# A mixture-of-experts layer's spare block: 64 rows with high and low parts side by side in place of 128 rows in three passes

## The reference

```python
xn = layernorm(x)                                   # x: (4, 1024, 512), 4096 rows
x + attention(xn) + moe(xn)

# moe: 8 experts, top 2 of softmax(xn @ Wg); capacity C = 1280 rows an expert
dispatched = xr[dispatch_mask.reshape(-1) % S].reshape(E, C, d)
h = jax.nn.relu(jnp.einsum('ecd,edf->ecf', dispatched, w1))      # d = 512, f = 2048
expert_out = jnp.einsum('ecf,efd->ecd', h, w2)
out = jnp.einsum('ks,ksm->sm', combine_weights, rerouted)
```

## Time and profile before

| | us |
|---|---|
| median of 3 runs | 2025.3 |
| lowest, highest | 2024.24, 2025.47 |
| profiled execution, its own time | 2021.71 |
| its span, first to last instruction | 2020.0 |
| TensorE busy | 2002.4 (99%) |
| VectorE busy | 906.2 (45%) |
| ScalarE busy | 553.9 (27%) |
| GpSimd busy | 722.8 (36%) |

### The profile page before, as it was taken

One profiled execution on the slowest core, in us unless ns is written; L12 is line 12 of the kernel. 1 busy time (PEld: TensorE's weight loads), 2 busy tenths in 40 slices (PEclk: granted clock), 3 DMA queues, 4 the chain that ended last, 5 costly groups with the idle time before them and its releaser, 6 DMA issues.

```text
span 2020.0 us, 29149 instructions
## 1 busy us (share of the span) xinstructions
PE 2002.4 (99%) x11768; PEld 1655.5 (82%) x11768; DVE 906.2 (45%) x1792; ACT 553.9 (27%) x986; POOL 722.8 (36%) x600
## 2 busy tenths in 40 slices
PE   9999999999999999999999999999999999999998
PEld 7888888878888888888888888888888888888887
DVE  8777677767752234224333422432352235324311
ACT  6322232223242123123212312321242124123211
POOL 4545544554442324323232431332143214333311
PEclk9999999999999999999999999999999999999999
DMA  6112121202341124215233421521152116223121
GB/s 201 68 64 86 39 69 64 86 28 80 127 151 29 44 60 143 43 58 114 66 68 70 132 44 54 125 67 35 47 146 54 28 47 160 44 63 86 56 32 21
DMA packets 85506, 151.46 MB, mean 75 GB/s; under 512 B 18304, under 2 KB 18304, under 8 KB 85360
## 3 DMA queue, kind: packets, MB, share of 16 engines
q1 hardware_dynamic: 61312, 105.64, 16.2%
q0 software_dynamic: 24048, 43.76, 12.5%
HBM read 109.82 MB, written 39.53 MB: 74 GB/s over the span
## 4 chain that ended last, share of the span: by engine, by line
PE 97%; DVE 1%; issue 0%; DMA 0%; SPq 0%; POOL 0%; ACT 0%; DVEq 0%; POOLq 0%
PE bank L1266 48%; PE bank L1570 34%; PE bank L1402 4%; PE bank L1320 2%; PE bank L1625 2%; PE bank L1391 2%; PE bank L1273 1%; PE bank L1385 1%; PE bank L1355 1%; PE bank L1294 1%; PE bank L1365 1%; DVE stats L891 0%; DMA attn_raw<-in_L_attn_Wv 0%; DMA x_in<-in_L_attn_x 0%; PE bank L1414 0%
## 5 line engine op out<-in xcount | busy, mean ns | idle before, releaser
L1213 DVE SCALAR_TENSOR_TENSOR h_lo<-bank,h_hi 128x512 fp32r<-128x512 f32 x254 | 175.3, 690 | 738.4 <-ACT h_hi L848 703.3
L637 POOL DMA_INDIRECT gathered<-xn_rows,gather_row x304 | 321.3, 1057 | 474.2 <-DVE x_blocks L1068 293.1
L1266 PE MATMUL bank<-xT_hi,w_hi 128*128 128x512 f32 x1024 | 399.1, 390 | 0.6 <-issue 0.5
L1266 PE MATMUL bank<-xT_hi,w_lo 128*128 128x512 f32 x1024 | 398.7, 389 | 0.0
L1266 PE MATMUL bank<-xT_lo,w_hi 128*128 128x512 f32 x1024 | 398.7, 389 | 0.0
L1570 PE MATMUL bank<-w_hi,h_hi 128*128 128x512 f32 x1016 | 395.6, 389 | 0.0
L1570 PE MATMUL bank<-w_hi,h_lo 128*128 128x512 f32 x1016 | 395.5, 389 | 0.0
L1570 PE MATMUL bank<-w_lo,h_hi 128*128 128x512 f32 x1016 | 395.5, 389 | 0.0
L848 ACT ACTIVATE h_hi<-bank 128x512 fp32r<-128x512 f32 x254 | 151.7, 597 | 789.5 <-PE bank L1266 744.6
L650 POOL DMA_INDIRECT out_rows<-y,add_row x80 | 128.9, 1611 | 546.7 <-ACT y L841 473.1
L1266 PEld LDWEIGHTS bank<-xT_hi,w_hi 128*128 128x128 f32 x1024 | 192.3, 188 | 41.8 <-issue 2.0
(11 more groups left out here) (217 smaller groups left out, 2324.6 us busy)
## 6 DMA issues: line engine op xcount, KB each, us to landing
raw_weights<-in_L_ffn_w SPq DMA_DIRECT2D x256, 256.0 KB
x_in<-in_L_attn_x SPq DMA_DIRECT2D x32, 256.0 KB
xn_rows<-xn SPq DMA_DIRECT2D x32, 256.0 KB, 2.8
x_res<-in_L_attn_x SPq DMA_DIRECT2D x32, 256.0 KB
out_rows<-y_attn SPq DMA_DIRECT2D x28, 256.0 KB
gathered<-xn_rows,gather_row POOLq DMA_INDIRECT x304
out_rows<-y,add_row POOLq DMA_INDIRECT x80, 5.7
attn_raw<-in_L_attn_Wq SPq DMA_DIRECT2D x4, 256.0 KB, 5.2
```

The source lines that it names most:

```text
L637: pool.indirect_dma_start(xg[:, nth % 2, q * P:(q + 1) * P], None, xn_pieces, bass.IndirectOffsetOnAxis(ap=gather_row[:, col, q:q + 1], ax ...
L1213: v_.scalar_tensor_tensor(lo[:, 0:n * P], h_bank[f % 2][:, 0:n * P], 0.0, hi[:, 0:n * P].bitcast(F32), ALU.max, ALU.subtract).then_inc(S[" ...
L1266: last = mm(dest, at(left[l], t), at_r(right[r], t), start=(i == 0), stop=(i == n - 1))
```

## The change

The first spare block now covers 64 rows. Its rows are kept as `x_halves`: for each of two halves of the tile, 64 columns of high parts and 64 columns of low parts side by side, one stationary operand of 128 columns. One pass with the high weights and one with the low weights give, in the two halves of the bank's partitions, the products of the high and of the low parts (so low by low is computed too). ScalarE copies the bank without the Relu, TensorE turns it as before, VectorE adds the two halves (a reduce over pairs, into `x_blocks`), ScalarE takes the Relu of the sum as high part, VectorE the rest as low part, both written side by side into `h_hi`, and the down product again takes two passes. Of its output bank, ScalarE scales the partitions 64 to 127 and VectorE scales the others and adds.

The second spare block is entered past 1088 rows in place of 1152. It does the other 64 rows of the first tile in the same way (`half_spare`), and then the second tile's 128 rows with three passes as before (`whole_spare`), into bank 1. It has two scatters. The gates and row numbers of the first tile are also stored with the partition halves swapped.

```diff
+HALF = P // 2
+PIECES = {1: FCHUNKS, 2: 2 * FCHUNKS}
+Y_SLOTS = [[0, 1, 2, 3], [0], [0, 1], [0, 1, 2, 3]]
...
+            if j == 1:
+                x_halves = esb("x_halves", [P, 2, DT, 2 * HALF], F32R)
...
-            return done + [(f"spare_y_by_act{k}", e + (0 < k < j)) for k in range(1, LAST)]
+            return done + [(f"spare_y_summed{k}", e + (k < j)) for k in range(1, LAST)] + [("spare_tile_out", e + (j == LAST))]
...
+            first = slot_gate[:, COLUMN[1]:COLUMN[1] + 1]
+            return (first[near, :], swapped_gate[far, :]) if j == 1 else (swapped_gate[near, :], first[far, :])
...
+        def half_cols(h, part):
+            return x_halves[:, h, :, part * HALF:(part + 1) * HALF].rearrange("p t (q c) -> p t q c", q=QUADS // 2)
+        def half_blocks(h):
+            return by_k_tile(x_blocks)[:, :, h * QUADS // 2:(h + 1) * QUADS // 2, :]
+        def by_part(ap):
+            return ap.rearrange("p (f part s) -> p f part s", f=FPC, part=2)
+        def h_sum(c):
+            return x_blocks[:, c % 2 * FPC * HALF:(c % 2 + 1) * FPC * HALF].rearrange("p (f s) -> p f s", f=FPC)
...
+                    col = COLUMN[1] if j == 1 else SLOT_TILES
+                    pool.wait_ge(S[f"spare_y_summed{j}"], e + 1)
+                    pool.indirect_dma_start(out[:, :], bass.IndirectOffsetOnAxis(ap=add_row[near, col:col + 1], axis=0),
+                                            y[near, 0, :], None, compute_op=ALU.add).then_inc(y_added[0], 16)
+                    if j == 2:
+                        col = COLUMN[2]
+                        pool.wait_ge(S["spare_tile_out"], e + 1)
+                        pool.indirect_dma_start(out[:, :], bass.IndirectOffsetOnAxis(ap=add_row[:, col:col + 1], axis=0),
+                                                y[:, 1, :], None, compute_op=ALU.add).then_inc(y_added[1], 16)
...
-                for i in range(BLOCKS[j]):
-                    uses = [sum(n > i for n in BLOCKS[:k]) for k in (j + 1, len(BLOCKS))]
+                for i in Y_SLOTS[j]:
+                    uses = [sum(i in slots for slots in Y_SLOTS[:k]) for k in (j + 1, len(BLOCKS))]
...
+                if j == 1:
+                    a.copy(half_cols(0, 0), half_blocks(0))
+                    a.copy(half_cols(1, 0), half_blocks(1)).then_inc(S["xT_hi_made"], 1)
...
-                            act.wait_ge(S[f"spare_h_done{j}"], FCHUNKS * e + c + 1)
-                            a.activation(xg[:, c % 2, :], h_bank[c % 2][:, :], ACT.Relu).then_inc(S[f"spare_h_ready{j}"], 1)
+                            act.wait_ge(S[f"spare_h_done{j}"], first + c + 1)
+                            a.copy(xg[:, c % 2, :], h_bank[c % 2][:, :]).then_inc(S[f"spare_h_ready{j}"], 1)
                         if c > 0:
-                            wait(act, (f"spare_turned{j}", FCHUNKS * e + c))
-                            a.copy(h_hi[(c - 1) % 2][:, :], xt_bank[(c - 1) % 2][:, :]).then_inc(S[f"spare_hi_made{j}"], 1)
-                    rows_out(j)
-                expert_blocks(act, e, main, spare, (("spare_h_ready", FCHUNKS), ("spare_hi_made", FCHUNKS), ("spare_y_by_act", 1)))
+                            wait(act, (f"spare_h_summed{j}", FCHUNKS * e + c))
+                            a.activation(by_part(h_hi[(c - 1) % 2][:, :])[:, :, 0, :], h_sum(c - 1), ACT.Relu
+                                         ).then_inc(S[f"spare_hi_made{j}"], 1)
+                    act.wait_ge(S["add_rows_ready"], e + 1)
+                    wait(act, (f"spare_y_done{j}", j * e + 1), ("adds_over", len(BLOCKS) * e + j))
+                    a.activation(y[near, 2, :], y_bank[0][far, :], ACT.Copy, scale=half_gates(j)[1]).then_inc(S[f"spare_far_out{j}"], 1)
...
+                if j == 1:
+                    v_.tensor_tensor(half_cols(0, 1), half_blocks(0), half_cols(0, 0).bitcast(F32), ALU.subtract)
+                    v_.tensor_tensor(half_cols(1, 1), half_blocks(1), half_cols(1, 0).bitcast(F32),
+                                     ALU.subtract).then_inc(S["xT_lo_made"], 1)
...
-                        v_.tensor_scalar(spare_used[:, 1, :], taken[0:1, :], float(MAIN + P), None, ALU.is_gt).then_inc(S["spare_known"], 1)
+                        v_.tensor_scalar(spare_used[:, 1, :], taken[0:1, :], float(MAIN + HALF), None, ALU.is_gt).then_inc(S["spare_known"], 1)
...
+                            v_.tensor_copy(swapped_gate[far, :], slot_gate[near, COLUMN[1]:COLUMN[1] + 1])
+                            v_.tensor_copy(swapped_gate[near, :], slot_gate[far, COLUMN[1]:COLUMN[1] + 1])
+                            v_.tensor_copy(add_row[near, SLOT_TILES:], slot_rec[far, COLUMN[1], 0:1])
+                            v_.tensor_copy(add_row[:, 0:SLOT_TILES], slot_rec[:, :, 0]).then_inc(S["add_rows_ready"], 1)
...
+                def half_spare(j):
+                    first = PIECES[j] * e
+                    for c in range(FCHUNKS):
+                        h_both, turned = by_part(h_hi[c % 2][:, :]), by_part(xt_bank[c % 2][:, :])
+                        dve.wait_ge(S[f"spare_turned{j}"], first + c + 1)
+                        v_.tensor_reduce(h_sum(c), turned.rearrange("p f part s -> p f s part"), AX.X, ALU.add
+                                         ).then_inc(S[f"spare_h_summed{j}"], 1)
+                        dve.wait_ge(S[f"spare_hi_made{j}"], first + c + 1)
+                        v_.scalar_tensor_tensor(h_both[:, :, 1, :], h_sum(c), 0.0, h_both[:, :, 0, :].bitcast(F32),
+                                                ALU.max, ALU.subtract).then_inc(S[f"spare_lo_made{j}"], 1)
+                    dve.wait_ge(S[f"spare_far_out{j}"], e + 1)
+                    v_.scalar_tensor_tensor(y[near, 0, :], y_bank[0][near, :], half_gates(j)[0],
+                                            y[near, 2, :], ALU.mult, ALU.add).then_inc(S[f"spare_y_summed{j}"], 1)
...
-                            product(h_bank[c % 2][:, :], (xT_hi[j], xT_lo[j]), (w1_hi[c], w1_lo[c]), DT,
-                                    slab).then_inc(S[f"spare_h_done{j}"], 1)
+                            for t in range(DT):
+                                for w in (w1_hi, w1_lo):
+                                    last = mm(h_bank[c % 2][:, :], x_halves[:, j - 1, t, :], w[c][:, t, :],
+                                              start=(t == 0 and w is w1_hi), stop=(t == DT - 1 and w is w1_lo))
+                            last.then_inc(S[f"spare_h_done{j}"], 1)
...
                             for f in range(FPC):
+                                for w in (w2_hi, w2_lo):
+                                    last = mm(y_bank[0][:, :], h_hi[d % 2][:, f * P:(f + 1) * P], w[d][:, f, :],
+                                              start=(d == f == 0 and w is w2_hi), stop=(d == FCHUNKS - 1 and f == FPC - 1 and w is w2_lo))
+                    last.then_inc(S[f"spare_y_done{j}"], 1)
```

More of the change, by code:

```diff
@@ L270, in expert_blocks @@
                 with eng.Else():
-                    for name, count in skipped:
-                        eng.sem_inc(S[f"{name}{1 + i}"], count)
+                    for name, count in skipped(1 + i):
+                        eng.sem_inc(S[name], count)
             main(LAST)
@@ L307, in evicted, with half_gates @@
             done = [("y_by_act", main_added(BY_ACT, e, j)), ("y_by_dve", main_added(BY_DVE, e, j))]
-            return done + [(f"spare_y_by_act{k}", e + (0 < k < j)) for k in range(1, LAST)]
+            return done + [(f"spare_y_summed{k}", e + (k < j)) for k in range(1, LAST)] + [("spare_tile_out", e + (j == LAST))]
+        near, far = slice(0, HALF), slice(HALF, P)
+        def half_gates(j):
+            first = slot_gate[:, COLUMN[1]:COLUMN[1] + 1]
[8 more added lines that the diff above has]
+            return x_blocks[:, c % 2 * FPC * HALF:(c % 2 + 1) * FPC * HALF].rearrange("p (f s) -> p f s", f=FPC)
         def split_units(j, f, follows):
@@ L480, in _ @@
             for i, s in enumerate(y_added):
-                sp.wait_ge(s, 16 * EXPERTS * sum(n > i for n in BLOCKS))
+                sp.wait_ge(s, 16 * EXPERTS * sum(i in slots for slots in Y_SLOTS))
         @block.gpsimd
@@ new lines, in half_spare, with whole_spare @@
+                    act.wait_ge(S["add_rows_ready"], e + 1)
+                    wait(act, (f"spare_y_done{j}", j * e + 1), ("adds_over", len(BLOCKS) * e + j))
+                    a.activation(y[near, 2, :], y_bank[0][far, :], ACT.Copy, scale=half_gates(j)[1]).then_inc(S[f"spare_far_out{j}"], 1)
+                def whole_spare():
+                    first = PIECES[2] * e + FCHUNKS
+                    for c in range(FCHUNKS + 1):
+                        if c < FCHUNKS:
+                            act.wait_ge(S["spare_h_done2"], first + c + 1)
+                            a.activation(xg[:, c % 2, :], h_bank[c % 2][:, :], ACT.Relu).then_inc(S["spare_h_ready2"], 1)
+                        if c > 0:
+                            wait(act, ("spare_turned2", first + c))
```

(35 more changed lines are left out.)

66 lines of the change are left out of this document (44 added, 22 removed).

## The result

| | before | after |
|---|---|---|
| median, us (runs) | 2025.11 (6) | 2014.47 (6) |
| lowest, highest | 2024.24, 2026.53 | 2012.0, 2016.3 |
| ratio, 95% interval | | 0.9943 [0.9932, 0.9953] |
| profiled execution, span | 2021.71, 2020.0 | 2012.0, 2010.3 |
| TensorE busy, matmuls | 2002.4, 11768 | 1982.4, 11672 |

Faster, by 10.6 us: half of the 21.4 that the prediction gave, and 6 us above the upper end of its range.

A forecast was written before the change was run, and what follows sets the result against it. TensorE's streaming of matmul columns was taken to bound the kernel. Terms of -21.8 for matmuls and +0.3 for the chain gave -21.4 us (unrounded terms), so 2000.3 profiled and 2004.0 us timed, range 2000.5 to 2008.5.

The forecast's parts named there:

- Matmuls of a used block: Two passes in place of three in both projections: 32 fewer matmuls, 7.25 us less per used block, 21.8 for three.
- The chain behind a turn: VectorE reduce, ScalarE Relu, VectorE subtract after TensorE's transposes: last chunk waits 0.1 us a block, 0.3 in all.
- rival A: The reduce is slow and TensorE waits on that chain: 2.7 us in place of 0.3, 2006.4 us; chance 0.08.
- The block's end: ScalarE copies half the output bank's partitions, VectorE adds the rest; TensorE needs the bank later: cost nothing.
- small steps: In every expert, splitting the first spare block's turned rows adds about 0.2 us each on ScalarE and VectorE: cost nothing.
- one more scatter: GpSimd issues one more scatter per expert, 1.55 us and 0.3 between two, under cover: cost nothing.
- Skipped blocks: TensorE's jumps over unused spare blocks, 80 + 192 matmuls and turns for 2 x 112: taken as 0, at most 4 us.
- Rival B: Longer jumps stall TensorE: 2008 us at 0.5 us more in eight experts, 2020 at 2 us each; chance 0.06.
- Rival D: TensorE pays for the removed pass elsewhere, something else closing the block; half the gain kept, 2014 us; chance 0.03.
- From the profile to the median: Timed median 3.6 us above the profiled execution; the same difference added to 2000.3 gives 2003.9 us.
- no new hole in experts 3, 0, 4 and 5 at the jump beyond 0.1 us: Sign of being right: TensorE shows no added idle time beyond 0.1 us at those experts' jumps over spare blocks.
- the two signs of being wrong: Blocks shrink to 16.5 us but the span falls by less than 19 us; or the reduce reads 1 us or more.

The follow-up runs named there:

- before_again: The kernel before, unchanged, profiled and timed a second time: 2025.31 us, ratio 0.9998.
- before_one: The kernel before without the second spare block's code, its semaphores counted up unconditionally: 2024.36 us, ratio 0.9991.
- before_long: The kernel before with 48 never-executed matmuls added to the second spare block, 544 instructions jumped over: 2033.39 us, ratio 1.0036.
- before_hints: The kernel before with the second block's test nested in the first's code and hints on both TensorE branches: 2004.8 us, ratio 0.9992.
- after_again: The changed kernel, unchanged, profiled and timed a second time: 2012.53 us, ratio 0.9935 to the kernel before.
- after_one: The changed kernel without the second spare block's code, its semaphores counted up unconditionally: 2001.85 us, ratio 0.9885 to the kernel before.
- after_hints: The changed kernel with the second block's test nested in the first's code and hints on both TensorE branches: 1983.88 us, ratio 0.9889.
- before_longer: The kernel before with 112 never-executed matmuls added to the second spare block, 672 instructions jumped over: ratio 1.0053.
- after_nested: The changed kernel with the second block's test inside the first block's code, so unused blocks take one jump: 2012.61 us, ratio 0.9934.
- after_hint: after_nested with TensorE's outer branch written by hand and hinted ahead of the main block's last matmuls: 2007.01 us, ratio 0.9904.

## Why the prediction was wrong

The timed span splits in three: until the first spare block starts, from there to TensorE's last matmul without the holes, and the holes.

| profile | first block at | rest without holes | holes |
|---|---|---|---|
| before | 635.43 | 1376.8 | 1.0 |
| before_again | 639.21 | 1376.7 | 1.5 |
| before_one | 639.47 | 1376.3 | 0 |
| before_long | 639.85 | 1376.9 | 7.1 |
| before_hints | 619.89 | 1376.3 | 0 |
| after | 639.49 | 1355.8 | 8.3 |
| after_again | 638.24 | 1356.0 | 10.5 |
| after_one | 637.11 | 1355.0 | 0 |
| after_hints | 619.97 | 1355.4 | 0.5 |

(After: the last matmul starts at 2003.58, and 2003.58 - 639.49 - 8.3 = 1355.8.)

- *Matmuls of a used block*: right. 96 matmuls fewer, 7.11 us a block; the middle column falls by 20.7 to 21.3 us in its four pairs (before and after, again, one, hints).
- *The chain behind a turn*: right. 0.11 us where 0.1 was given; the reduce took 0.69 us for the 0.68 of its nearest row, so rival A did not happen.
- *The block's end, small steps, one more scatter*: right at nothing. No wait of TensorE after names a scatter or the half tile's copies; VectorE's new step took 0.74 us for 0.69.
- *Skipped blocks*: this step failed. I wrote "I take 0: expert 3 shows that the jump as such can be free". Measured: 8.3 and 10.5 us of holes in place of 1.0 and 1.5, so 7 to 9 us more; my upper bound of 4 us came from one hole of 0.5 us at the old distance. What the runs show in the place of a free jump is a wait for code: TensorE goes on 1.8 to 2.3 us after a packet of 256 instructions has landed, and at the new distance a second packet can stand behind the first. A row of the old length says nothing of a longer jump when the cost comes in a step, and the step lies just there, between 496 and 544. The rule that I had put beside it and not priced in, of a stall when a branch leaves a window of two blocks of 256 instructions (the Trainium skill, "Runtime: NRT & Kernel Launch", section "Instruction fetch mechanics"), gives an estimate for the step: a jump over more than 512 instructions always leaves the window. The runs agree with it for jumps over both blocks; the larger buffer for TensorE that the same section gives does not show here. Rival B had the mechanism, at 0.06. Its near price (0.5 us each, 2008) was too low and its far one (2 us in all eight experts, 2020) too high: six places at 1.4 us each on average in the first profile. Rival D names 2014 us, almost the measured time, but that is luck: its mechanism, a scatter or a weight load that closes the block, would have kept the blocks long, and all three shrank by 7.11 us.
- *From the profile to the median*: the profiled execution was short by 3.6 us, and I carried the difference over. That was right for before. Where it lies is now seen: 635.43 against 639.21 in the first column, that is in attention, which the change does not touch; 3.1 us of it are waits for "issue" (6.1 against 9.2 us).
- *The sum by its measured terms*: -21.0 in the middle column (1355.8 - 1376.8), +7 for the holes, 14 us less; with the second pair -20.7 and +9, 12 us less. The two sets of timed runs gave 10.6 and 13.3; the spans fell from 2024.0 (before_again) to 2010.3 and 2011.4. So the second set fits, and the first is 3 us off. Of these, 2.5 us are that the profiled execution, 2012.0, was the shortest of its six runs (2012.0 to 2016.3); where the longer ones lose it, no trace shows.
- *What would show it*: of the signs that I named, "no new hole in experts 3, 0, 4 and 5 at the jump beyond 0.1 us" failed, at experts 3 and 5, and one of the two signs of being wrong came true: the blocks shrank to 16.5 us and the span fell by less than 19 us (2020.0 to 2010.3).

Left open: why TensorE's step behind expert 5's used block, at a jump over 384 instructions, takes 1.2 to 2.7 us and the same jump in experts 0 and 4 costs nothing, when jumps over 320 (before_long) and 448 (before_longer) there cost 0 to 0.3. The packets narrow it down. In after_nested one starts 0.5 to 0.6 us ahead of the last matmul of the block in experts 0, 4 and 5 alike; TensorE's step ends 2.0 us after its landing in expert 5, and there is no wait in experts 0 and 4. So the length of the jump does not decide here. Where the target lies within the 256 instructions of a packet may; no run moved it by itself.

## What to carry to other kernels

Code that a branch jumps over is part of a change's price, even if it never runs: count the instructions between a branch and its target, weight loads included, before and after, and treat a count that crosses a limit as a rival with a real chance, because here the price came as a step. Where the outcome of a branch is known early, tell the engine so ahead of independent work; here it gave back all of the loss, in a kernel where TensorE sets the time and every wait of it counts. And take a second profile of the kernel before, or use the timed spread, before reading 4 us off one execution.

## What the runs showed of the hardware

- A jump of TensorE over 448 or 496 instructions costs 0 to 0.6 us, over 544 some 0.3 to 2.3 us in one step, which lies at the target or two to five matmuls behind it, over 672 about 2 us. Matmuls behind it can come at 0.43 us for 0.23, six or seven in a row; with these an expert has lost up to 4 us (expert 1 of after_nested).
- The wait goes with a DMA packet of 256 instructions, which takes about 1 us, or 1.8 to 2.4 behind another one: TensorE's first matmul starts 1.8 to 2.3 us after its landing (37 steps), and a wait at a matmul further behind the target ends 1.2 to 1.4 us after a landing (7 steps).
- A hint on the branch, ahead of the last matmuls before it, takes the wait away, for an outer and an inner branch (five holes of after_nested gone in after_hint, expert 5's in after_hints), and does no harm where the block is used: the three used blocks start without a wait in both.
- TensorE's waits for "issue" in attention come on some chips only. On the chips of the first two sets the first spare block starts at 637 to 641 us and these waits are 7.6 to 9.6 us before it; on the third they are 0 and it starts at 620, in all three kernels profiled there (before_hints, below); the kernel before takes 2006.39 us on it, 19 less. The holes behind a jump over 672 instructions exist on this chip too. The waits in attention are another thing than the holes: the same 45 packets arrive before the first spare block on every chip, and most of these waits, where there are any, end 6 to 12 us after the last landing. Their cause is open.

```profile
PE bank L1444 <- POOL ident L524: 2.7, 1, 2.7
PE bank L1414 <- DVE scores L956: 1.0, 1, 1.0
PE bank L1296 <- DVE scores L956: 0.3, 1, 0.3
PE bank L1362 <- DVE takes L990: 0.3, 1, 0.3
```
